# Products without use on TensorE in the attention loop: 36 of 384 columns ahead of each group's logits, 8 of 252 ahead of its maxima

## The reference, cut to what matters

```python
logits = leaky_relu(a_src[src_all] + a_dst[dst_all] + a_edge, 0.2)
m = segment_max(logits, dst_all)
p = exp(logits - m[dst_all])
denom = segment_sum(p, dst_all)
out = segment_sum((p / denom[dst_all])[:, :, None] * x_l[src_all], dst_all)
```

## Time and profile before

| | us |
|---|---|
| median of 3 runs | 4684.2 |
| lowest and highest run | 4669.44, 4692.47 |
| the profiled execution | 4726.66 |
| its span | 4724.8 |

### The profile page before, as it was taken

One profiled execution on the slowest core, in us unless ns is written; L12 is line 12 of the kernel. 1 busy time (PEld: TensorE's weight loads), 2 busy tenths in 40 slices (PEclk: granted clock), 3 DMA queues, 4 the chain that ended last, 5 costly groups with the idle time before them and its releaser, 6 DMA issues. The chain is left out here.

```text
span 4724.8 us, 62095 instructions
## 1 busy us (share of the span) xinstructions
PE 2421.1 (51%) x19840; PEld 2026.5 (43%) x19840; DVE 2595.8 (55%) x6998; ACT 1606.2 (34%) x2523; POOL 1917.0 (41%) x1972
## 2 busy tenths in 40 slices
PE   3689999999889233333333333333333333333333
PEld 2567777787777233222323323232223232332333
DVE  2679998757764444444444444444444444444447
ACT  1477778745556122222222222222222222222221
POOL 4411113212232555445444444455445454444552
PEclk9989999999999555555555555555555555555555
DMA  3233337528887222222221222222222222222223
GB/s 114 80 126 144 145 149 167 162 82 259 246 243 249 93 53 53 52 53 53 53 53 51 52 56 52 52 53 53 52 53 53 52 53 52 52 54 54 53 54 73
DMA packets 167882, 431.68 MB, mean 91 GB/s; under 512 B 42680, under 2 KB 91376, under 8 KB 159204
## 3 DMA queue, kind: packets, MB, share of 16 engines
q1 hardware_dynamic: 57672, 269.90, 15.4%
q0 software_dynamic: 66640, 129.84, 14.0%
q10 hardware_dynamic: 43244, 27.80, 2.0%
HBM read 308.86 MB, written 120.11 MB: 91 GB/s over the span
## 5 line engine op out<-in xcount | busy, mean ns | idle before, releaser
L2220 POOL DMA_INDIRECT G<-x_tab,idx x1611 | 1522.7, 945 | 1553.4 <-ACT idx L2271 995.5
L2411 DVE TENSOR_TENSOR ACC<-pu,ACC 128x140 f32 x1641 | 488.9, 298 | 606.1 <-DMA at_in<-in_edge_attr 409.1
L2359 PE MATMUL pc<-ident,SCR 60*128 60x60 f32 x108 | 35.2, 326 | 1487.5 <-DVE SCR L2531 1476.9
L2318 PE MATMUL pu<-MSG,OH 128*128 128x140 f32 x3282 | 767.3, 408 | 27.2 <-issue 20.1
L2318 PEld LDWEIGHTS pu<-MSG,OH 128*128 128x128 f32 x3282 | 700.1, 300 | 37.1 <-issue 26.2
L2359 PEld LDWEIGHTS pc<-ident,SCR 60*128 60x128 f32 x108 | 19.1, 177 | 1494.5 <-issue 1494.5
L2528 DVE SCALAR_TENSOR_TENSOR SCR<-SCR,pc 60x128 f32<-60x128 f32 x108 | 37.5, 347 | 907.2 <-remote 905.4
L961 ACT CAST AE<-psA 128x784 bf16<-128x784 f32 x496 | 396.6, 815 | 181.2 <-PE psA L994 137.7
L2283 ACT ACTIVATE pq<-DL 128x60 f32<-128x60 f32 x108 | 24.2, 225 | 1111.2 <-DVE DL L2538 1111.2
L1095 DVE TENSOR_TENSOR OHL<-iol,LH 128x2048 bf16<-128x2048 bf16 (+1 forms) x248 | 358.5, 1445 | 75.6 <-PE psA L994 33.1
L1005 PE MATMUL psR<-SPL,AE 128*128 128x384 bf16 x1736 | 328.7, 329 | 9.9 <-issue 9.9
(11 more groups left out here) (432 smaller groups left out, 4690.0 us busy)
## 6 DMA issues: line engine op xcount, KB each, us to landing
a_tab<-AE SPq DMA_DIRECT2D x62, 1568.0 KB
OHT<-rel_tab SPq DMA_DIRECT2D x108, 480.0 KB, 3.6
AE<-a_tab SPq DMA_DIRECT2D x60, 800.0 KB
AE<-a_tab SPq DMA_DIRECT2D x60, 768.0 KB
G<-x_tab,idx POOLq DMA_INDIRECT x1611
at_in<-in_edge_attr SPq DMA_DIRECT2D x26, 250.0 KB
SUMS<-in_edge_attr ACTq DMA_DIRECT2D x24, 250.0 KB
ae_t<-room ACTq DMA_DIRECT2D x13, 256.0 KB
```

Of the source, the lines that this page charges most:

```text
L2220: pool.indirect_dma_start(G[:, u % 4, j, :], None, x_tab, bass.IndirectOffsetOnAxis(ap=idx[:, u % 4, j:j + 1], axis=0)).then_inc(s_g[u % 4 ...
L2318: mm = pe.matmul(pu[:, k[0], k[1]:k[1] + MW], OH[:, u % 4, j, :], MSG[:, u % 2, j, :], start=True, stop=True)
L2411: dve.tensor_tensor(a, pu[:, k[0], k[1]:k[1] + MW][:, None, :], a, ALU.add).then_inc(s_c, 1)
```

## The change

Ahead of each step on TensorE stands a wait for the turned keys of the step before (`s_kc`), and then 36 products of bfloat16, with 128 columns of `REL` as weights and 384 others as the moving side, into bank 1 of `pt`, columns 0 to 383. Ahead of the wait for the joined maxima stand 8 such products of 252 columns into `px`, columns 260 to 511. Nothing reads what they write, and they signal nothing.

```diff
+                def keep_warm(out, times):
+                    for _ in range(times):
+                        pe.matmul(out, REL[:, 0:P], REL[:, P:P + out.shape[1]], start=True, stop=True)
+
                 def step(i, u, g, left):
+                    pe.wait_ge(s_kc, g + 1)
+                    keep_warm(pt[:, 1, 0:3 * P], 36)
                     hold(pe, s_l, g + 2)
                     pe.transpose(pl, L[:].rearrange("p h j -> p (h j)"), ident[:]).then_inc(s_lt, 1)
...
                     if left != 0:
                         spread(g + 1, u + 1, range(4))
+                    keep_warm(px[:, 2 * P + HEADS:4 * P], 8)
                     hold(pe, s_r, g + 1)
                     pe.transpose(pc[:, 192:192 + R], CM, ident[0:R, 0:R]).then_inc(s_rt, 1)
```

## The result

Four executions of the changed kernel gave a median of 4914.6 us (4902.2 to 4919.2), four of the kernel before 4681.7 us (4669.4 to 4692.5): a ratio of 1.0494 with a 95% interval of 1.0461 to 1.0527, so 233 us or 5% slower. The profiled execution took 4919.2 us (span 4917.0) against 4726.7 (span 4724.8) before: 192 us apart. The remaining 40 are the 45 us by which the profiled execution of before stood above its median (after's stands 5 above).

What follows compares the result with a forecast made beforehand. Groups were taken to be bound by TensorE signals released only when the gathers are through. 0.6 x 0.7 + 0.4 x 2.8 = 1.5 us over 104 groups gave 160; 4684 + 160 = 4844 us, range 4480 to 5260.

Steps and rivals of the forecast that it cites:

- The bound: Group loop: beside gathers TensorE's signal comes out only when they are through, 21.5 us after their start; group 28.7 us.
- The burst: 36 products ahead of the logits' turn: 8.6 us, 3.9 of it covered by TensorE's wait, so turn 4.7 us later.
- The turn's signal: Signal of the turned logits, now deep among the gathers: may be 6.6 us late, the turn 4.8 us behind their start.
- The worst case: Turned logits released only 21.5 us after the gathers' start: group 35.8 us, +7.1 us a group.
- the rival in which the whole chain falls behind the gathers: Turn's signal waits behind the 36 products' PSUM writes: +7.1 us a group, 5422 us; whole or part, 17 in 100.
- The late case: Rows of maxima not out before gathers end, released at 21.5 us: +2.2, with second burst +2.8; four groups in ten.
- The two cases: Rows of maxima out before gathers end, +0.7 us, or not, +2.8; weighted 0.6 and 0.4, 1.5 us a group.
- The early case: Rows of maxima get out before the gathers end: +0.7 us, a group of 29.4 us; six groups in ten.
- The second burst: 8 products ahead of the joined maxima: 1.7 us at half clock, free in a usual group, 0.6 us late otherwise.
- The clock: Higher clock shortens TensorE's products mostly where they have cover: gain 0 to 0.3 us a group, costed as none.
- The sign: Whole kernel: slower by over 0.5% 60 in 100, within 0.5% 15, faster 25.

Runs made afterwards that it cites:

- the 36 alone: The change without its eight second products, against the kernel before: 4855.0 us, ratio 1.0364 on chip 11; 3526.4 (0.9993) on chip 5, 3525.8 (0.9984) on chip 3.
- The eight alone: The change without its 36 products, only the 8 ahead of the maxima, against the kernel before on chip 5: 3531.3 us, ratio 1.0003.
- the ten: Ten products instead of 36 ahead of the turn of the logits and no eight, against the kernel before on chip 5: 3526.7 us, ratio 0.9995.
- the 36 behind the turn: The 36 products moved behind the turn of the logits and no eight, against the kernel before on chip 5: 3945.3 us, ratio 1.1182.

## Why the prediction was right, point by point

*The bound.* Right where it was made: the groups were tied to the moment at which TensorE's signals come out behind the gathers, and that moment did not move. In the trace of before it let DVE go on with the maxima 21.5 us behind the gathers' start, in this one with the rows of maxima at 21.2. The gathers take 18.5 us from first start to last end (3029.41 to 3047.88), 18.4 before. That holds for the slow level; on the fast one no signal is held and POOL's gathers are the bound.

*The burst.* 8.6 us were taken for the 36. The group above has 7.5, and over the 108 groups of the changed kernel the median is 7.7 and the mean 8.1. The turn stood 4.3 us behind the gathers' start against 4.8 in the prediction.

*The turn's signal.* The worst case had it held to 21.5 us. It was prompt, 4 to 5 us behind the start, so the rival in which the whole chain falls behind the gathers did not come. The late case had counted on this signal too: 4.8 for the turn, 6.6 for its late signal, 2.4 to the rows' product and 9.7 for the rows' own lateness, 23.5 together. What came was 4.3, nothing, 1.5 and 15.4 (3033.69 and 3035.19, read at 3050.60). The sum was too late for the gathers either way, but it was made up otherwise than I had it.

*The two cases.* Both exist. The early case was read from the earlier trace rows as a group of 29.4 us and is 29.3. The late one was priced 28.7 + 2.2 + 0.6 = 31.5 and is 30.9: the 2.2 are 2.28 in the timeline, the second burst costs 0.2 in a group that is late anyway. Two terms were mis-sized, and they pull opposite ways. Four groups in ten were given to the late case; of 96 groups off the back edge, 72 took it, and 7 more were in between. And that case was priced at 2.8 us and costs 2.2. With both as measured, 0.25 x 0.7 + 0.75 x 2.2 = 1.8 us a group, and 1.90 is measured. With the share alone put right the sum would have been 0.25 x 0.7 + 0.75 x 2.8 = 2.3, some 237 us over 104 groups, so that the forecast of 1.5 came as near as it did is in part luck. The median lies 71 us above 4844, inside the range. Of these, 32 come from the groups (with 11 us the other way from the stages ahead): the profiled execution was forecast at 4887 and took 4919. The rest is that the profiled execution of before stood 42 us above the median it was given with, and that of the change only 5.

*The second burst.* It was forecast free in six groups of ten and 0.6 us in the others, 0.24 on the average. It cost (30.26 - 29.69) = 0.57 on the average; 29.69 is (4811.5 - 1634.9)/107 of the 36 alone. In the counts it works less by its length than by turning early groups into late ones; how it does that no run shows.

*The clock.* Forecast at no gain, and on the slow level none is to be seen: from the maxima to the next start of the gathers the group above takes 7.5 us (3052.88 to 3060.34), against 7.2 before. L2318, the chunk sums, did become shorter, 325 ns against 409 in the mean of the loop. Most of them lie beside the gathers, where there is cover.

*What the prediction did not have.* Nothing in one trace could say that its level was one of two. The sign it gives holds for chip 11 and for the chip of the first comparison. Its terms all come from a trace of the slow level, and that the result was taken on that level too is what let it come true. On chips 3 and 5 the parts of the change moved the time by less than 0.2%; the whole change was not run there, so that it makes no difference on that level is expected from its parts and not shown.

*What stays open.* Why TensorE's signals are held back at one level and never at the other is not known. Each comparison on the slow level held the changed kernel, and each on the fast one did not, so by these runs the chip and something in the comparison can't be told apart; two of the three slow ones were on chip 11, the first one's chip is not recorded. The eight alone, the ten and the 36 behind the turn ran on the fast level only, so whether it is the burst's time or its writes in PSUM that costs on the slow level is not separated either. The kernel before was not run on chip 11 without the change beside it, nor the change on chip 3, 5 or 9. Nor is it shown that gathers by index are what holds the signals on the slow level, since the kernels without them ran on chip 9 alone, where nothing was held. The expectation that told DMA writes from gathers by index was met at 3169 us there, but it could not have failed on a level without held signals. The slow traces themselves speak for the gathers. The last of the held signals comes out some 3 us behind the end of the last gather's issue in both, and in the earlier trace rows, with nothing left to gather, signals are prompt. And in the stages ahead of the loop the profile before has 26 waits of over 0.3 us that end by "remote". Of these 25 end while POOL issues an indirect DMA or at most 3.2 us behind it; such times make up 37% of the first 1550 us, and of DVE's and ACT's 445 other waits for TensorE there 33% end in them. In the changed kernel it is 23 of 24. That is a strong coincidence and not an experiment.

## What to carry to other kernels

Work without use put where an engine "waits anyway" is free only as far as the wait is slack at that very place, and here the slack was 4 us and the burst 8. What counts is not the engine's busy share but which step of the chain has been reached when the held signals come out: some 4 us of delay cost 0.6 us where the rows of maxima still got out early, and 2.2 where they did not. Ask for a second chip and a second comparison before believing the size of a wait that no instruction of the kernel explains.

## What the runs showed of the hardware that I had not expected

- The same kernel has two steady levels, near 4680 and near 3530 us. Per group it is 28.4 us against 18.6 ((3477.7 - 1491.8)/107, the kernel with idle instructions), and the stages ahead of the attention differ too: the first maxima come at 1643.7 and at 1491.8 us. The gathers' own pace, 1.25 us for 128 rows, is the same on both.
- On the slow level the turn's signal, sent 4.3 us behind the gathers' start, is prompt. The one of the rows of maxima is held for 10 us in the group where the product stands at 5.1 us, and for 15 us, until the gathers are through, in the groups where it stands at 5.8. The Trainium skill, "Perfetto Trace Analysis", section on TensorE in the per-engine timelines, has the signal go out once PSUM has acknowledged the writes; that leaves room for such a delay, and no run here shows that this is the step at which it arises.
- The held signals come out in steps. In the trace of the 36 alone 99 reads of the rows of maxima start more than 13 us behind the gathers' start, and 96 of them lie within 0.1 us of 13.45 plus a multiple of 0.70 (14.15, 14.85 and so on up to 21.15); in the changed kernel it is 94 of 98. What sets the step no run shows.
- Four or ten idle instructions of POOL between two indirect DMAs leave their distance at 1.25 us.
- Without gathers the bursts hold the mean grant at 0.93 against 0.65; beside them 0.70 against 0.58. Without gathers it then takes 6.6 us from the turn of the logits to the maxima (2608.32 to 2614.91) instead of 7.5 (2607.08 to 2614.59), which are also the medians of all groups. That is what the clock is worth to this part of the chain: under one us, for a burst of six.
